# Waiting for one row tile at a time at the turn to the second half of the rows

## The chip, the cores and the metric

The kernel runs on the 8 cores of one Trainium2 chip, in two dies of four. Each core computes 1024 of the 8192 rows; the weights are worked up on every core, and no core waits for another. The metric is device time in microseconds, of the slowest core, from one launch.

## The reference, cut to what matters

```python
def attn(x, w1, w2, b2, sparse_mask):
    a = jnp.einsum('ds,td->st', w1, w2) * sparse_mask          # 4096 x 4096
    return jax.nn.gelu(jnp.einsum('bds,st->bdt', x, a) + b2, approximate=False)

def ffn(x, qweight, scales, scaled_zeros, bias):
    w = (qweight * scales + scaled_zeros).reshape(4096, 4096)   # groups of 128
    return jnp.einsum('bsi,oi->bso', x, w) + bias

x = x + 0.5 * ffn(layernorm(x), ...)
x = x + attn(layernorm(x), ...)
x = x + 0.5 * ffn(layernorm(x), ...)                            # x: 1 x 8192 x 4096, f32
```

## The kernel before

**Two stages.** The first, up to about 1350 us, makes the two weight matrices in bf16 in DRAM: amat, the masked product of w1 and w2, and wdqT, the dequantised and transposed qweight. The second, which the change touches, runs the three layers over the core's rows.

**The second stage.** The loop over u takes 512 rows at a time, as NT = 4 tiles of 128 rows (index j) that lie side by side in x_sb, 4096 f32 columns each. There is one x_sb; both halves use it. Per u three passes p follow one another: p = 0 and p = 2 are the ffn, p = 1 is attn. A pass is a LayerNorm of the four tiles and then matmuls in 8 output blocks (oc) of 512 columns. In the matmuls the four tiles have a PSUM bank each, with 32 products of 128x128 by 128x512 per tile and block for p = 0 and 2; the moving operand mv is double buffered, 4 MB in each half.

**The LayerNorm of one tile.** ScalarE makes the sum of x in p = 0 (L503, a copy with an accumulator) and of its squares (L510), each over 4096 columns, and, after three small instructions of VectorE, the square root (L516). VectorE takes the reciprocal (L618), writes the normalised tile into h_tmp (L623) and then copies 32 transposed blocks from PSUM to hT (L634), while TensorE transposes them (L546), four blocks ahead at most. h_tmp is single, so tile j+1 is normalised when tile j is transposed. ScalarE runs ahead: it works on tile j+1 when its square root of tile j is done. TensorE's first matmul of a pass (L566) waits for all 128 copies, for mv_ld and for the PSUM banks.

**The turn from u = 0 to u = 1.** The last evictions of u = 0 (L648) finish x_sb tile by tile. In SyncE's queue stand four stores of y (L481), each behind the eviction of its tile, each with a semaphore of its own, st_o[j]. Behind them stand the loads of mv for u = 1 (L472); the first two wait for nothing that is not yet done. GpSimd has four loads of the next x tiles into the same places (L428), each behind a wait for its st_o[j]. All four increment one semaphore, x_ld2, by 16 each. ScalarE waits at j = 0 for x_ld2 at 64, and likewise, then without effect, at j = 1 to 3.

Of the kernel before, what the change touches and what calls it, by code (L numbers as in the profile page):

```python
# [24 lines left out]
def A_base(u, p, j):  # L25
    return u * 28 + sum(4 * cA(q) for q in range(p)) + j * cA(p)

def V_base(u, p, j):
    return u * 68 + sum(4 * cV(q) for q in range(p)) + j * cV(p)
# [4 lines left out]
def G_base(u, p):  # L34
    return (u * 3 + p) * 8

def E_base(u, p):
    return (u * 3 + p) * 32
# [79 lines left out]
def build_nc():  # L118
# [21 lines left out]
    def sem1(name):  # L140
        return es.enter_context(nc.semaphore(name))

    def semn(name, n):
        return [es.enter_context(nc.semaphore(f"{name}{i}")) for i in range(n)]
# [23 lines left out]
    mk_ld = semn("mk_ld", 2)  # L168
    p1_st = semn("p1_st", 2)
    x_ld = sem1("x_ld")  # L170
    x_ld2 = sem1("x_ld2")
    st_o = semn("st_o", 4)
    mv_ld = semn("mv_ld", 2)

    with es:
# [7 lines left out]
        with nc.Block() as block:  # L183
            from contextlib import ExitStack as _ES

            with _ES() as es_1:
# [154 lines left out]
                @block.scalar  # L341
                def _(s):
                    acts = []
                    for qq, (sb, tc) in enumerate(P_PAIRS):
                        if TC_FIRST[qq]:
                            acts.append((K_BEFORE[qq], 0, qq))
                    for r in range(32):
                        acts.append((QW_POS[r] + 4, 1, r))
                    for _, kind, idx in sorted(acts):
                        if kind == 0:  # L350
                            qq = idx
                            tc = P_PAIRS[qq][1]
                            sl2 = (qq % 2) * NC * 512
                            s.wait_ge(wt_ld[qq % 2], WT_CNT[qq])
                            s.dma_start(
                                out=w2b.rearrange("(c p) t -> p c t", p=128)
                                    [:, :, tc * 512:(tc + 1) * 512],
                                in_=w2t[:, sl2:sl2 + NC * 512]
                                    .rearrange("p (c t) -> p c t", t=512),
                            ).then_inc(wb_st[tc], 16)  # L360
                        else:
                            r = idx
                            s.wait_ge(wqev, 32 * (r + 1))
                            s.dma_start(out=wdqT.rearrange("(c p) o -> p c o", p=128)
                                        [:, :, r * 128:(r + 1) * 128],
                                        in_=asm2[:, (r % 2) * D:(r % 2) * D + D]
                                        .rearrange("p (c o) -> p c o", o=128)
                                        ).then_inc(q_st[r % 2], 16)
# [43 lines left out]
            with _ES() as es_2:  # L412
# [11 lines left out]
                @block.gpsimd  # L424
                def _(g):
                    for j in range(NT):
                        g.wait_ge(st_o[j], 16)
                        g.dma_start(  # L428
                            out=x_sb[:, j * D:(j + 1) * D],
                            in_=x_in[512 + j * 128:512 + (j + 1) * 128, :],  # L430
                        ).then_inc(x_ld2, 16)

                @block.sync
                def _(sync):
# [54 lines left out]
                @block.scalar  # L489
                def _(s):  # L490
                    for _tc in range(8):
                        s.wait_ge(wb_st[_tc], 16)
                    for u in range(2):
                        for p in range(3):
                            for j in range(NT):
                                a0 = A_base(u, p, j)
                                v0 = V_base(u, p, j)
                                s.wait_ge(ac_ln, a0)
                                if p == 0:
                                    s.wait_ge(x_ld if u == 0 else x_ld2, 64)  # L500
                                    if u == 1:
                                        s.wait_ge(p2_ev, 96)
                                    s.activation(sq_scr[:], x_sb[:, j * D:(j + 1) * D],  # L503
                                                 AF.Copy,
                                                 accum_out=stats[:, j:j + 1]
                                                 ).then_inc(ac_ln, 1)
                                    s.wait_ge(ac_ln, a0 + 1)
                                else:
                                    s.wait_ge(p2_ev, E_base(u, p - 1) + 29 + j)
                                s.activation(sq_scr[:], x_sb[:, j * D:(j + 1) * D],  # L510
                                             AF.Square,
                                             accum_out=stats[:, 4 + j:5 + j]
                                             ).then_inc(ac_ln, 1)
                                tvar_idx = 3 if p == 0 else 4
                                s.wait_ge(ve_ln, v0 + tvar_idx)
                                s.activation(stats[:, 16 + j:17 + j],  # L516
                                             stats[:, 4 + j:5 + j],
                                             AF.Sqrt,
                                             bias=stats[:, 12 + j:13 + j],
                                             scale=1.0 / D).then_inc(ac_ln, 1)  # L520
                            if p == 1:
                                for oc in range(8):
                                    for j in range(NT):
                                        l = oc * 4 + j
                                        s.wait_ge(p2_pe, G_base(u, 1) + oc + 1)
                                        if l >= 2:
                                            s.wait_ge(p2_ev, E_base(u, 1) + l - 1)
                                        s.activation(  # L528
                                            gel[:, (l % 2) * 512:(l % 2) * 512 + 512],
                                            psb[j][:],  # L530
                                            AF.Gelu).then_inc(p2_gl, 1)
# [153 lines left out]
```

## Time and profile before

| | us |
|---|---|
| median of 2 runs | 3017.17 (3008.67 and 3025.67) |
| the profiled execution | 3009.43 |
| its span on the slowest core, core 6 | 3007.9 |
| TensorE busy, matmuls | 1872.3 |
| VectorE busy | 755.8 |
| ScalarE busy | 168.3 |
| first instruction of the second stage on ScalarE | 1349 |
| turn to u = 1, last eviction to first matmul | about 2144 to 2245 |

A span runs from the first to the last instruction of a core. Busy times are sums over one engine; a line number names the line of the kernel from which an instruction came. "Idle before, released by" tells what an engine had waited for. "Us to landing" is the time of a DMA from its issue until its last byte has arrived, so that issue plus this time is the moment at which its semaphore is complete.

### The profile page before, as it was taken

What the parts mean: (1) busy time and instruction counts of PE and PEld (TensorE: products, weight loads), DVE (VectorE), ACT (ScalarE), POOL (GpSimd) and SP (SyncE); (2) the same over time, 40 slices, a digit from 0 to 9 for tenths busy, and PEclk for the clock granted to TensorE, in tenths of its full rate; (3) what the DMA queues carried; (4) which work ended last, traced back from release to release, by engine and by line L of the source; (5) the groups of instructions that cost most, each with busy time, mean ns of one, the idle gap of its engine ahead of it and who ended that gap; (6) DMA issues with size and microseconds to landing.
All of it is one profiled execution on the core that took longest, in us unless ns stands there. A gap on an engine that the chain in (4) does not pass through costs nothing.

```text
span 3007.9 us, 25494 instructions; the slowest of 8 cores (2980.3 to 3007.9 us)
## 1 busy us (share of the span) xinstructions
PE 1872.3 (62%) x8280; PEld 844.1 (28%) x8280; DVE 755.8 (25%) x3395; ACT 168.3 (6%) x157; POOL 83.1 (3%) x124
## 2 busy tenths in 40 slices
PE   0554166340755506736899665999449986758996
PEld 0222023120322202313333322333124333223332
DVE  0033144330553413634100425000040004241000
ACT  0000000000000000003000212000040002130000
POOL 1000000000000000000000000000000000000000
PEclk9977577665776757766889676999759996768898
DMA  9998989999799898962342023333553330241442
GB/s 157 188 173 192 175 116 163 143 216 157 110 161 182 200 170 129 187 194 89 126 144 77 16 71 112 112 112 112 176 160 112 112 113 22 65 121 62 144 130 112
DMA packets 402702, 399.49 MB, mean 133 GB/s; under 512 B 135696, under 2 KB 370992, under 8 KB 396432
## 3 DMA queue, kind: packets, MB, share of 16 engines
q0 software_dynamic: 57856, 117.37, 25.5%
q1 hardware_dynamic: 180240, 213.39, 23.8%
q10 hardware_dynamic: 164480, 67.11, 10.6%
q8 instruction: 72, 1.18, 0.2%
q14 instruction: 54, 0.44, 0.1%
HBM read 407.47 MB, written 91.10 MB: 166 GB/s over the span
## 4 chain that ended last, share of the span: by engine, by line
PE 50%; DMA 15%; another core or an unknown queue 15%; DVE 13%; issue 5%; ACT 2%; DVEq 1%; SPq 0%; ACTq 0%; POOLq 0%
PE ps L566 37%; DMA amat<-aev 8%; PE pa L400 8%; DMA mkt<-mask 4%; DVE x_sb L648 3%; DVE wout L309 3%; DVE asm L333 2%; DVE hT L634 2%; PE tr L546 2%; DVE h_tmp L623 2%; PE ptr L379 2%; PE ps L576 2%; DMA x_sb<-x_in 1%; DMA y_out<-x_sb 1%
## 5 line engine op out<-in xcount | busy, mean ns | idle before, releaser
L566 PE MATMUL ps<-mv,hT 128*128 128x512 bf16 x4536 | 1098.8, 409 | 142.0 <-DVE x_sb L648 137.4
L566 PEld LDWEIGHTS ps<-mv,hT 128*128 128x128 bf16 x4536 | 467.0, 104 | 772.0 <-issue 312.9
L400 PE MATMUL pa<-w2t,w1blk 128*128 128x512 bf16 x1760 | 441.1, 416 | 351.7 <-DMA w1blk<-w 240.6
L379 PE MATMUL ptr<-ident_bf,wout 128*128 128x128 bf16 x1024 | 163.1, 241 | 363.5 <-DVE asm L333 352.1
L400 PEld LDWEIGHTS pa<-w2t,w1blk 128*128 128x128 bf16 x1760 | 182.5, 105 | 596.8 <-issue 429.3
L648 DVE SCALAR_TENSOR_TENSOR x_sb<-ps,x_sb 128x512 f32<-128x512 f32 x128 | 80.8, 687 | 1007.5 <-PE ps L576 1007.5
L546 PE MATMUL tr<-ident_bf,h_tmp 128*128 128x128 bf16 x768 | 131.6, 264 | 255.3 <-DVE h_tmp L623 242.4
L309 DVE TENSOR_SCALAR wout<-qt,scl_sb,zro_sb 128x128 bf16<-128x128 bf16 x1024 | 234.0, 318 | 26.0 <-DMA qt<-qw 26.0
L321 DVE TENSOR_TENSOR aev<-pa,mkt 128x512 bf16<-128x512 f32 x55 | 37.8, 689 | 729.7 <-PE pa L400 435.1
L379 PEld LDWEIGHTS ptr<-ident_bf,wout 128*128 128x128 bf16 x1024 | 100.2, 100 | 431.2 <-issue 395.0
L333 DVE COPY asm<-ptr 128x128 bf16<-128x128 bf16 x1024 | 165.5, 218 | 42.2 <-DMA wdqT<-asm 20.8
L546 PEld LDWEIGHTS tr<-ident_bf,h_tmp 128*128 128x128 bf16 x768 | 80.3, 105 | 308.1 <-issue 288.5
L634 DVE COPY hT<-tr 128x128 bf16<-128x128 bf16 x768 | 124.0, 219 | 35.0 <-PE tr L546 18.4
L510 ACT ACTIVATE sq_scr<-x_sb 128x4096 bf16<-128x4096 f32 x24 | 86.8, 3616 | 563.3 <-DVE x_sb L648 560.5
L648 DVE SCALAR_TENSOR_TENSOR x_sb<-gel,x_sb 128x512 f32<-128x512 f32 x64 | 41.7, 690 | 172.5 <-ACT gel L528 172.5
L503 ACT ACT_TABLE_LOAD x1 | 1.3, 1283 | 1349.2 <-DMA x_sb<-x_in 1349.2
L232 POOL DMA_DIRECT2D amat<-aev x55 | 30.3, 550 | 1156.2 <-DVE aev L321 853.7
L623 DVE TENSOR_SCALAR h_tmp<-x_sb,stats 128x4096 bf16<-128x4096 f32 x24 | 57.9, 2412 | 4.6 <-DVE stats L618 4.6
L503 ACT ACTIVATE sq_scr<-x_sb 128x4096 bf16<-128x4096 f32 x8 | 28.9, 3616 | 332.7 <-DMA x_sb<-x_in 331.6
L528 ACT ACTIVATE gel<-ps 128x512 f32<-128x512 f32 x64 | 36.4, 596 | 156.1 <-PE ps L576 149.0
L576 PE MATMUL ps<-fb_bf,halves_bf 1*128 1x512 bf16 x128 | 33.0, 377 | 0.0
L603 DVE TENSOR_SCALAR stats<-stats 128x1 f32<-128x1 f32 x24 | 3.6, 151 | 116.4 <-ACT sq_scr L510 115.1
(32 smaller groups left out, 134.9 us busy)
## 6 DMA issues: line engine op xcount, KB each, us to landing
mv<-wdqT SPq DMA_DIRECT2D x32, 4096.0 KB, 14.0
w1blk<-w POOLq DMA_DIRECT2D x16, 2048.0 KB, 55.1
w2t<-w2T POOLq DMA_DIRECT2D x8, 4096.0 KB, 59.4
w2b<-w2t ACTq DMA_DIRECT2D x8, 4096.0 KB, 44.1
qt<-qw POOLq DMA_DIRECT2D x32, 1024.0 KB, 16.0
wdqT<-asm ACTq DMA_DIRECT2D x32, 1024.0 KB, 13.5
w2t<-w2b SPq DMA_DIRECT2D x6, 4096.0 KB, 49.5
y_out<-x_sb SPq DMA_DIRECT2D x8, 2048.0 KB, 16.1
```

The lines of the kernel that those rows point to most:

```text
L309: v.tensor_scalar(wout[:, sl * D + gg * 128: sl * D + gg * 128 + 128], qt[:, sl * D + gg * 128: sl * D + gg * 128 + 128], scl_sb[:, r * 32 ...
L321: v.tensor_tensor(aev[:, (k % 2) * 512:(k % 2) * 512 + 512], pa[k % 2][:], mkt[:, (k % 2) * 512:(k % 2) * 512 + 512], op=ALU.mult,).then_i ...
L333: v.tensor_copy(asm2[:, (r % 2) * D + blk * 128: (r % 2) * D + blk * 128 + 128], ptr[b % 4][:],).then_inc(wqev, 1)
L379: t.transpose(ptr[b % 4][:], wout[:, (r % 2) * D + blk * 128: (r % 2) * D + blk * 128 + 128], ident_bf[:]).then_inc(wqtr, 1)
L400: ins = t.matmul(pa[k % 2][:], w1blk[:, dc * 1024 + st * 128: dc * 1024 + st * 128 + 128], w2t[:, (qq % 2) * NC * 512 + dc * 512: (qq % 2) ...
L510: s.activation(sq_scr[:], x_sb[:, j * D:(j + 1) * D], AF.Square, accum_out=stats[:, 4 + j:5 + j]).then_inc(ac_ln, 1)
L546: t.transpose(trp[tg % 4][:], h_tmp[:, ic * 128:(ic + 1) * 128], ident_bf[:]).then_inc(p2_tr, 1)
L566: t.matmul(psb[j][:], hT[:, ic * 512 + j * 128: ic * 512 + j * 128 + 128], mv[:, sl + ii * 512:sl + ii * 512 + 512], start=(ii == 0), stop ...
L576: ins = t.matmul(psb[j][:], lrow[0:1, :], brow[0:1, oc * 512:(oc + 1) * 512], start=False, stop=True,)
L623: v.tensor_scalar(h_tmp[:], x_sb[:, j * D:(j + 1) * D], stats[:, 8 + j:9 + j], stats[:, 20 + j:21 + j], op0=ALU.subtract, op1=ALU.mult).th ...
L634: v.tensor_copy(hT[:, ic * 512 + j * 128: ic * 512 + j * 128 + 128], trp[tg % 4][:],).then_inc(p2_trv, 1)
L648: v.scalar_tensor_tensor(x_sb[:, j * D + oc * 512: j * D + oc * 512 + 512], src, 1.0, x_sb[:, j * D + oc * 512: j * D + oc * 512 + 512], o ...
```

## The change

The one semaphore of the four loads becomes four, and ScalarE waits at tile j for the load of tile j alone. The first half of the rows keeps its single wait for all four tiles. Nothing else differs; loads, stores and their order are as before.

```diff
-    x_ld2 = sem1("x_ld2")
+    x_l2 = semn("x_l2", 4)
...
                             in_=x_in[512 + j * 128:512 + (j + 1) * 128, :],
-                        ).then_inc(x_ld2, 16)
+                        ).then_inc(x_l2[j], 16)
...
                                 if p == 0:
-                                    s.wait_ge(x_ld if u == 0 else x_ld2, 64)
+                                    if u == 0:
+                                        s.wait_ge(x_ld, 64)
+                                    else:
+                                        s.wait_ge(x_l2[j], 16)
                                     if u == 1:
                                         s.wait_ge(p2_ev, 96)
```

## Rows read from the trace of the kernel before

**Rows 1.** Spans and granted TensorE clock of the cores, slowest and fastest

```profile
core 5: 2980.3 us, clock 0.768
core 6: 3007.9 us, clock 0.764
```

**Rows 2.** Chain that ended last, core 6: start us, us, what

```profile
2180.68 13.94 DMA x_sb<-x_in
2194.76 3.72 ACT sq_scr L503 x2
...
2245.13 29.53 PE ps L566 x128
```

**Rows 3.** Timeline, core 6, GpSimd: start us, us, instruction [idle before]

```profile
2151.61 0.54 POOL L428 DMA_DIRECT2D x_sb<-x_in  x1 [844.86 <-DMA y_out<-x_sb]
2160.23 0.54 POOL L428 DMA_DIRECT2D x_sb<-x_in  x1 [8.09 <-DMA y_out<-x_sb]
2170.74 0.53 POOL L428 DMA_DIRECT2D x_sb<-x_in  x1 [9.96 <-DMA y_out<-x_sb]
2180.68 0.53 POOL L428 DMA_DIRECT2D x_sb<-x_in  x1 [9.41 <-DMA y_out<-x_sb]
```

**Rows 4.** Timeline, core 6, SyncE's queue: the first two mv loads, same columns

```profile
2146.20 55.64 SPq L472 DMA_DIRECT2D mv<-wdqT  x2
```

**Rows 5.** DMA issues, core 6 (x tiles, then mv): us to landing last

```profile
x_sb<-x_in POOLq DMA_DIRECT2D x1, 2048.0 KB, 18.5
...
x_sb<-x_in POOLq DMA_DIRECT2D x1, 2048.0 KB, 19.7
...
x_sb<-x_in POOLq DMA_DIRECT2D x1, 2048.0 KB, 16.2
...
x_sb<-x_in POOLq DMA_DIRECT2D x1, 2048.0 KB, 13.9
...
mv<-wdqT SPq DMA_DIRECT2D x1, 4096.0 KB, 64.9
```

**Rows 6.** Timeline, core 6, ScalarE: the starts of tiles 1 and 3

```profile
2203.64 3.62 ACT L503 ACTIVATE sq_scr<-x_sb 128x4096 bf16<-128x4096 f32 x1 [0.20 <-ACT stats L516]
...
2224.82 3.62 ACT L503 ACTIVATE sq_scr<-x_sb 128x4096 bf16<-128x4096 f32 x1 [0.20 <-ACT stats L516]
```

**Rows 7.** Timeline, core 6, VectorE: tile 0, then tile 1

```profile
2202.37 0.15 DVE L603 TENSOR_SCALAR stats<-stats 128x1 f32<-128x1 f32 x1 [57.99 <-ACT sq_scr L510]
...
2203.88 2.41 DVE L623 TENSOR_SCALAR h_tmp<-x_sb,stats 128x4096 bf16<-128x4096 f32 x1 [0.18 <-DVE stats L618]
...
2212.99 0.14 DVE L603 TENSOR_SCALAR stats<-stats 128x1 f32<-128x1 f32 x1
```

**Rows 8.** Stretches, core 6, first LayerNorm: busy us, PEclk, DMA share, GB/s

```profile
1362.00:1373.00 11.00, 5.85 (x36) 3.69 (x36) 8.23 (x40) 8.54 (x6) 0.00 (x0) 0.50 1.07 343
1373.00:1384.00 11.00, 5.84 (x34) 3.40 (x33) 8.46 (x40) 7.91 (x7) 0.00 (x0) 0.50 0.07 23
```

**Rows 9.** Core 1: loads of tiles 0, 1, us to landing, ScalarE's start

```profile
2129.43 0.54 POOL L428 DMA_DIRECT2D x_sb<-x_in  x1 [832.61 <-DMA y_out<-x_sb]
2134.58 0.54 POOL L428 DMA_DIRECT2D x_sb<-x_in  x1 [4.61 <-DMA y_out<-x_sb]
...
x_sb<-x_in POOLq DMA_DIRECT2D x1, 2048.0 KB, 18.7
...
x_sb<-x_in POOLq DMA_DIRECT2D x1, 2048.0 KB, 25.9
...
2178.41 3.62 ACT L503 ACTIVATE sq_scr<-x_sb 128x4096 bf16<-128x4096 f32 x1 [331.68 <-DMA x_sb<-x_in]
```

**Rows 10.** Stretches, core 6, first matmuls behind the LayerNorm (L566)

```profile
2245.00:2246.00 1.00, 0.87 (x3) 0.35 (x4) 0.50 0.00 0
2250.00:2254.00 4.00, 4.00 (x21) 1.77 (x19) 1.00 0.00 0
```

**Rows 11.** Waits, core 6, 2245 to 3008 us, the longest: total, times, longest

```profile
DVE x_sb L648 <- PE ps L576: 503.2, 16, 31.7
```

## The prediction

> **What bounds the kernel now.** I read the spans of all cores first, then the page's part with slices of the span, then the chain of work that ended last around the turn from the first 512 rows to the second, and then the timelines of the queues in that stretch. The cores differ by under 1% in span, at one clock [rows 1], so the time is that of core 6 and every core can be argued alike. Behind 1350 us TensorE is what the kernel is made of, except at one place: the turn. There the chain leaves TensorE, goes through a store of y, then through the last load of x, then to ScalarE, and returns to the matmuls at 2245.1 us [rows 2]. The edit touches what ScalarE waits for in exactly this chain.
>
> The turn on core 6 runs so. GpSimd issues the four x loads one by one, each as the store of the same tile has landed: at 2151.6, 2160.2, 2170.7 and 2180.7 us [rows 3]. Two mv loads of 4 MB stand in SyncE's queue from 2146.2 us on, and share the DMA engines with them [rows 4]. The x loads take 18.5, 19.7, 16.2 and 13.9 us [rows 5], and so land at 2151.6+18.5 = 2170.1, 2160.2+19.7 = 2179.9, 2170.7+16.2 = 2186.9 and 2180.7+13.9 = 2194.6 us. ScalarE starts on tile 0 at 2194.8 [rows 2], 0.2 us behind the fourth landing: the wait for 64 is what held it, although its own tile had been there for 24.5 us.
>
> **What the change removes.** Tile 0 no longer waits for tiles 1 to 3. It can start at 2170.1+0.2 = 2170.3 us: 2194.8-2170.3 = **24.5 us** earlier. The rest of the LayerNorm follows tile 0 in a fixed order, one tile behind the other, and the question is whether the later tiles are there in time.
>
> ScalarE's first pass over tile 1 started at 2203.6 and over tile 3 at 2224.8 us [rows 6]; 24.5 us earlier these are 2179.1 and 2200.3. Tile 1 lands at 2179.9, so it is 0.8 us late. Tile 1 has room for that: ScalarE needs 2202.4-2194.8 = 7.6 us for its two passes over a tile [rows 2, 7], so it was through with tile 1 at 2203.6+7.6 = 2211.2, while VectorE, busy with tile 0, took it up at 2213.0 [rows 7]: 1.8 us of slack, more than 0.8. Tile 2, between them, was started half the way from tile 1 to tile 3, at about 2214.2; 24.5 us earlier that is 2189.7, and it lands at 2186.9, 2.8 us early. Tile 3 lands at 2194.6, 5.7 us early. So what sets the pace is VectorE, with one tile in about 10.6 us (2213.0-2202.4), and the whole row of work shifts by the full 24.5 us.
>
> **Does it keep its pace?** It now runs while x and mv are still landing, where before its second half had the DMA engines idle. The first LayerNorm of the kernel shows both: in the stretch with a DMA share of 1.07 VectorE was busy 8.23 us of 11.0, in the next, at a share of 0.07, 8.46 us of 11.0, with 40 instructions in each [rows 8]. DMA traffic doesn't stretch these instructions; I take zero. The bound above: 0.2 us in 11, or 1 us over the 50.4 us from 2194.8 to 2245.1.
>
> **What is late next.** At 2245.13-24.5 = 2220.6 us TensorE wants the first mv tile. It was issued at 2146.2 [rows 4] and landed 64.9 us later [rows 5], at 2211.1: 9.5 us to spare. The change issues no DMA and moves none, so this landing stays.
>
> **What it adds.** Three more waits on ScalarE, one for each of tiles 1 to 3. Behind each of them, in ScalarE's order, stand the two passes of the same tile and its square root, and behind those VectorE's normalisation, the transposes and so the matmuls. All of them need that tile anyway. The cost of a wait that is already met: nothing to a tenth of a microsecond (tile 1 started 0.2 us behind the square root in rows 6), covered by the slack above. Four semaphores in place of one: nothing that the trace would show. The wait on p2_ev for 96 is met at the end of the evictions, before the first load is issued.
>
> **The other cores.** Core 1 issued its first two x loads at 2129.4 and 2134.6; they took 18.7 and 25.9 us, and ScalarE started at 2178.4 [rows 9]. Tile 0 had landed at 2148.1, so it may gain 30.1 us with the same 0.2 us of wake-up. Tile 1, though, lands at 2160.5, and is wanted 8.9 us behind tile 0's start (2203.6-2194.8 on core 6), at 2157.2: 3.3 us late, 1.8 us of it covered, 1.5 lost. Core 1 gains 28.6. Core 6 was the last to reach the turn and its loads had the least company; it has the smallest gain and stays the last.
>
> **The sum.** 24.5 us off the span of core 6: 3007.9-24.5 = 2983.4. The profiled execution took 3009.43 us, 1.5 more than its span: 2984.9 us. One of the two runs shown is at 3008.67, like it, the other at 3025.67, and their median is 3017.17. I take the middle between the profiled execution and the median, 3013.3, as the base, and so 3013.3-24.5 = **2989 us**, 0.9% below the median. About 2%, some 60 us, is what a measurement of this kernel can tell from no change; by that measure this is no change.
>
> **Rivals.**
> *The fourth load is held up by VectorE.* New is that VectorE works on tile 0 while GpSimd still has a load to issue. VectorE's normalisation of tile 0, 2.41 us long from 2203.9 [rows 7], moves to 2179.4 to 2181.8, and the issue at 2180.7 falls into it. If the load had to wait for its end, it would come 1.1 us later, of the 5.7+1.8 = 7.5 us to spare: no loss. If it waited until VectorE is through with tile 0, at 2213.0-24.5 = 2188.5, it would land at 2202.4, 2.1 us late, 0.3 of it uncovered. If through tile 1 also (10.6 more), 10.9 us are lost: 3000 us. Against it: in the trace of before nothing of the sort is seen, as VectorE idled then. The Trainium skill, page "SBUF — State Buffer", section "Who interferes with whom", has a rule for it: a VectorE instruction in a two-port mode keeps GpSimd from a port that both use, for its whole length, and a DMA issued from GpSimd then waits for its descriptors. No row here shows it; by that rule the sum would be the first or the second of these cases, 2989 us either way. Chance of a loss of over 5 us: 5%.
>
> *mv gates the matmuls.* It would have to land 9.5 us later than it did. Each microsecond beyond costs one; at 10 beyond the time is 2999 us. For it speaks only that its landing is far longer than an undisturbed one, against it that all that it shares the engines with is issued at the same times as before. 3%.
>
> *TensorE's clock (the one that ends on the other side).* Its idle time at the turn shrinks. VectorE had idled 58.0 us ahead of tile 0 [rows 7], which becomes 33.5, and TensorE somewhat longer in both cases; its work ahead of the matmuls is the same. The first matmuls behind the LayerNorm ran at 0.50, the 1.2 GHz level, and within 5 us at 1.00, the 2.4 GHz level [rows 10]; so the first group of 128 took 29.5 us [rows 2], of which some 25 at the full clock. A group that stayed at the lower level would take 25 us more. One such group eats the gain (3013.3-24.5+25 = 3014 us), and from the fourth on (+100-24.5, 3089) the kernel is slower by over 2%. Nothing speaks for it: TensorE idles in both versions and starts its transposes at the lower level in this trace, and goes through the same 128 transposes. 2%.
>
> *The gain is lost later.* A later wait for a DMA would absorb it. The waits after 2245 us name none; the longest is VectorE's for the matmuls, 503.2 us [rows 11]. The stores at the end follow the last evictions. That the change does nothing at all (tile 0 in truth landing with tile 3) is against the landings of rows 5. Together 3%: about 3013 us.
>
> **Chances and range.** Forecast 87%, the four rivals 5, 3, 2 and 3%. Low end: the lowest run, 3008.67, less core 1's 30.1 and 3 us of spread: 2975. High end: the highest run less the gain is 3001, the first two rivals give 3000; with 5 us of spread, 3006. The cases beyond hold 5%, run-to-run spread perhaps 10 more. Faster by over 2% would need 36 us more than the turn holds here: 2%. Slower by over 2%: 2%. Within: 96%.
>
> **What would show it.** In the profile after, ScalarE's first L503 of the second half starts 0.2 us behind the landing of tile 0, some 24 us before the fourth lands; L503 waits for a DMA at tile 1, for about 1 us or a few on cores like core 1, and hardly at tiles 2 and 3; the four tiles keep 10.6 us each; TensorE's idle stretch ahead of the transposes shrinks by the same 24 us; the first matmul of the second half still waits for VectorE's hT and not for mv; the fourth load is issued and lands as before. The prediction would be wrong if the chain at that matmul named mv, if the fourth load took clearly over 14 to 19 us, or if the first matmul group took over 31 us.

## The result, and the profile after

The changed kernel took 2983.9 us, the median of 15 runs, against 3009.85 us for the kernel before in 14 runs of the same comparison: a ratio of 0.9909, with a 95% interval of 0.9876 to 0.9942. That is 26 us between the medians and 27 us by the ratio (17 to 37). A second comparison on another occasion, the run `again` below, gave 0.993 (0.9888 to 0.9971), some 21 us (9 to 34). The gain is clear of zero in both and short of 2%. All ratios leave out the runs in which the cores of a die ran at a lower TensorE clock (2 of the 15 here, one of the two of `sp_loads`, four of the seven of `cols_tail`), and since the profiles of `cols` and `cols_tail` below are of such runs, only the turn and the end, which come out alike on both dies, are read from them.

The profiled execution took 2978.37 us. Its spans, as in [rows 1]:

```profile
core 0: 2976.6 us, clock 0.767
...
core 6: 2964.1 us, clock 0.769
```

Core 0 ended last, not core 6. The chain of core 0 at the turn, start us, us, what, answering to [rows 2]:

```profile
2134.19 8.54 DMA y_out<-x_sb
2143.30 18.89 DMA x_sb<-x_in
2162.32 3.72 ACT sq_scr L506 x2
...
2212.69 29.58 PE ps L569 x128
```

The chain now runs over the store and the load of tile 0, where it ran over the last load. From the first load's issue it is 2143.3+18.9 = 2162.2 us, and ScalarE starts 0.1 us later. ScalarE's four first passes, as in [rows 6]:

```profile
2162.32 3.62 ACT L506 ACTIVATE sq_scr<-x_sb 128x4096 bf16<-128x4096 f32 x1 [307.58 <-DMA x_sb<-x_in]
...
2172.42 3.62 ACT L506 ACTIVATE sq_scr<-x_sb 128x4096 bf16<-128x4096 f32 x1 [1.41 <-DMA x_sb<-x_in]
...
2181.81 3.62 ACT L506 ACTIVATE sq_scr<-x_sb 128x4096 bf16<-128x4096 f32 x1 [0.20 <-ACT stats L519]
...
2192.39 3.62 ACT L506 ACTIVATE sq_scr<-x_sb 128x4096 bf16<-128x4096 f32 x1 [0.20 <-ACT stats L519]
```

The brackets tell what ended each wait: the DMA for tile 0, the DMA for tile 1 (1.41 us, where the start could have come 1.2 us sooner), and for tiles 2 and 3 only the square root ahead of them. VectorE, as in [rows 7]:

```profile
2169.94 0.15 DVE L606 TENSOR_SCALAR stats<-stats 128x1 f32<-128x1 f32 x1 [33.99 <-ACT sq_scr L513]
...
2180.55 0.14 DVE L606 TENSOR_SCALAR stats<-stats 128x1 f32<-128x1 f32 x1
...
2191.13 0.14 DVE L606 TENSOR_SCALAR stats<-stats 128x1 f32<-128x1 f32 x1
```

It idled 34.0 us ahead of tile 0 instead of 58.0, and takes up a tile every 10.6 us as before. No bracket stands at tiles 1 and 2: ScalarE's lateness with tile 1 did not reach it. So it is on cores 0, 2, 4 and 6, where VectorE's steps stay within 0.2 us of 10.6. On cores 1, 3, 5 and 7 tile 1 came later, and on 1, 3 and 7 tile 2 too: VectorE's steps there were 11.5 to 12.0 us and then 10.7 to 11.5, and the way from ScalarE's start to the first matmul took 51.5 to 52.7 us instead of 50.4 to 51.0.

For comparing runs I use the **turn**: from the issue of the first y store of the turn (L481) to the first matmul of the second half (L566, in the changed kernel L569), worked out for each core from the timelines. On core 0 after it is 2212.69-2134.19 = 78.5 us; on core 6 before 2245.1-2142.6 = 102.5.

| kernel | turn: shortest, median, longest core |
|---|---|
| before | 102.5, 106.4, 106.9 |
| changed | 76.9, 78.5, 80.6 |

Core by core the turn is shorter by 25.4 us (core 0), 27.8 (core 1), 24.6 (core 6) and 29.6 (core 7); the others lie between 26 and 29.

### The profile page after: what moved, and what is told of

Its sections match the earlier page's. It is cut to its first block, busy times and chain, and to the rows that moved or that the text cites. A ratio compares the mean times of both kernels' runs of the same rounds, so it can differ in the third digit from the quotient of the medians.

```text
span 2976.6 us, 25494 instructions; the slowest of 8 cores (2937.6 to 2976.6 us)
## 1 busy us (share of the span) xinstructions
PE 1873.3 (63%) x8280; PEld 844.5 (28%) x8280; DVE 753.8 (25%) x3395; ACT 168.3 (6%) x157; POOL 83.9 (3%) x124
## 3 DMA queue, kind: packets, MB, share of 16 engines
q10 hardware_dynamic: 164480, 67.11, 10.7%
## 4 chain that ended last, share of the span: by engine, by line
PE 50%; another core or an unknown queue 15%; DMA 14%; DVE 13%; issue 5%; ACT 2%; DVEq 1%; SPq 0%; ACTq 0%; POOLq 0%
PE ps L569 37%; PE pa L400 8%; DMA amat<-aev 7%; DMA mkt<-mask 5%; DVE x_sb L651 3%; DVE wout L309 3%; DVE asm L333 2%; DVE hT L637 2%; PE tr L549 2%; DVE h_tmp L626 2%; PE ptr L379 2%; PE ps L579 2%; DMA x_sb<-x_in 2%; ACT sq_scr L513 1%
## 5 line engine op out<-in xcount | busy, mean ns | idle before, releaser
L569 PE MATMUL ps<-mv,hT 128*128 128x512 bf16 x4536 | 1099.9, 409 | 141.9 <-DVE x_sb L651 137.3
L569 PEld LDWEIGHTS ps<-mv,hT 128*128 128x128 bf16 x4536 | 467.2, 104 | 772.7 <-issue 314.1
L637 DVE COPY hT<-tr 128x128 bf16<-128x128 bf16 x768 | 121.5, 219 | 36.7 <-PE tr L549 18.3
```

Source lines behind the costliest of these rows:

```text
L569: t.matmul(psb[j][:], hT[:, ic * 512 + j * 128: ic * 512 + j * 128 + 128], mv[:, sl + ii * 512:sl + ii * 512 + 512], start=(ii == 0), stop ...
L637: v.tensor_copy(hT[:, ic * 512 + j * 128: ic * 512 + j * 128 + 128], trp[tg % 4][:],).then_inc(p2_trv, 1)
```

## The experiments

Eight kernels ran. Times scatter by more than the differences looked for, since the cores come out of the first stage at times that differ from run to run (in `again` their first y stores were issued between 2050.8 and 2148.5 us, in the kernel before between 2117 and 2143), and the time is that of the last core. So the turn, which is read on eight cores in each profile, decides, and the ratio only confirms.

**The changed kernel again**, as a yardstick. No edit.

> The changed kernel once more, as the yardstick of this group. Turn means here: from the issue of the first y store of the first half to the first matmul (L569) of the second half. Theory (the turn is tile 0's landing plus a LayerNorm that VectorE paces at 10.6 us a tile): turn 77 to 81 us on every core, against 102 to 107 in the kernel before; time 24 to 29 us under the kernel before. Rival (part of the gain was luck of the cores' start times): turn shortened, but a time within 10 us of the kernel before.

Measured: turn 73.4, 76.2 and 77.2 us (shortest, median, longest), ratio 0.993 (0.9888 to 0.9971). The gain is there again, at some 21 us a little under the 24 to 29 expected. What I had not expected is how short the turn was on most cores, 73.4 us on core 7 and 73.8 on core 0: below my 77 to 81. The four x loads of core 7 took 15.9, 19.9, 15.2 and 11.5 us, where those of core 0 in the first profile took 18.9, 20.7, 17.1 and 15.1.

Core 7 came to its turn 24 us ahead of any other core, but that is not the reason. Core 3 had three others within 25 us of it, and its loads took the same 15.9, 19.9, 15.2 and 11.6 us. What both have is a distant neighbour in the pairs 0/1, 2/3, 4/5 and 6/7 (47 and 44 us later). Over the 48 cores of the six profiles in which GpSimd issues whole tiles, the four times add up to 78.9 to 89.6 us on all 17 cores whose neighbour began its turn between 3 us before and 21 us after them, and to 62.4 to 74.7 us on all 31 others. Six other ways to pair the cores (0/2, 0/4, 0/7 and so on) do not part them so.

**Tile 0 waits for tile 1 as well.**

```diff
                                         s.wait_ge(x_l2[j], 16)
+                                        if j == 0:
+                                            s.wait_ge(x_l2[1], 16)
```

> Tile 0 waits for its own load and for that of tile 1; tiles 2 and 3 as in the changed kernel. Theory: ScalarE starts at tile 1's landing, 10 to 12 us behind that of tile 0, all behind it shifts by as much: turn 88 to 91 us, time about 10 us over the changed kernel, some 15 under the kernel before. Rival (mv or the DMA traffic sets the turn, and tile 0's start only fills slack): turn under 84 us, time within 5 us of the changed kernel.

Measured: turn 82.3, 88.5 and 89.5 us, ratio 0.9955 (0.9912 to 0.9999), which by itself does not stand apart from that of `again`. The median turn is 12.3 us longer than that of `again`, which ran on the same chip, and ScalarE started 32 to 39 us behind the first store, where it started after 23 to 27. On core 4, the last of this run:

```profile
2182.73 3.62 ACT L508 ACTIVATE sq_scr<-x_sb 128x4096 bf16<-128x4096 f32 x1 [318.62 <-DMA x_sb<-x_in]
...
2191.61 3.62 ACT L508 ACTIVATE sq_scr<-x_sb 128x4096 bf16<-128x4096 f32 x1 [0.20 <-ACT stats L521]
...
2202.22 3.62 ACT L508 ACTIVATE sq_scr<-x_sb 128x4096 bf16<-128x4096 f32 x1 [0.20 <-ACT stats L521]
```

Only the first start waits for a DMA. What tile 0 waits is paid nearly in full at the first matmul: in the mean of the eight cores ScalarE starts 12.7 us later than in `again` and the turn is 12.1 us longer, since some cores of `again` had lost a little at tile 1. The rival (under 84 us) holds on no core but core 2, whose neighbour was 38 us behind it; against core 7 of `again` (73.4 us), whose neighbour was far off too, it lost 8.9 us, where ScalarE's start lost 9.2 (32.2 instead of 23.0).

**The first mv load ahead of the stores.** The load leaves its place in the loop behind the stores.

```diff
+                                if g == 24:
+                                    continue
...
+                        if u == 0:
+                            sync.wait_ge(p2_pe, 23)
+                            sync.dma_start(out=mv[...], in_=wdqT[...]).then_inc(mv_ld[0], 16)
                         for j in range(NT):
                             sync.wait_ge(p2_ev, E_base(u, 2) + 29 + j)
```

> The first mv load of the second half is issued ahead of the four y stores, when its buffer comes free at the end of matmul group 23, so that 4 MB less are moved in the turn. Theory: in SyncE's ring mv stood behind the stores and took nothing from tile 0's load; tile 0 lands 28 us behind the first store as before (within 1 us), turn 77 to 81 us, time as the changed kernel. Rival (mv shares the DMA engines with tile 0's load and holds it up): tile 0 lands 2 to 5 us sooner, turn and time shorter by as much.

Measured: turn 73.4, 75.7 and 78.3 us, ratio 0.9949 (0.9909 to 0.999). ScalarE started 23.0 to 27.8 us behind the first store, in `again` 23.0 to 26.5. On core 1 here and core 7 of `again` the loads took 15.9, 19.9, 15.1 and 11.5 against 15.9, 19.9, 15.2 and 11.5 us: the same without 4 MB of mv. mv takes nothing from tile 0. The trace before says why. On core 6 SyncE's queue moved this from 2142.6 us, the first store's issue, to 2180.6, where the fourth store had landed (packets, MB, share of the 16 engines):

```profile
q1 hardware_dynamic: 605, 8.42, 65.6%
```

8.42 MB are the four stores of 2.1 MB, all but 0.03, so mv, issued at 2146.2, had hardly begun. The prediction had it share the DMA engines with all four x loads.

**mv held until tile 3 has landed.**

```diff
+                                if g == 24:
+                                    sync.wait_ge(x_l2[3], 16)
                                 if g >= 2:
                                     sync.wait_ge(p2_pe, g - 1)
```

> The changed kernel, with SyncE's first mv load of the second half held until tile 3 of x has landed. Theory (mv has some 9.5 us of slack in the changed kernel, and stood behind the stores): tile 0's landing stays within 1 us, 23 to 28 us behind the first store; mv is issued 52 to 55 us behind the first store and needs 14 to 24 us, so it lands at 67 to 78, and the turn stays at 74 to 80 us. Rival (mv is the gate and slows x): x lands 3 us sooner or more, or the first matmul waits for mv and the turn moves with mv's landing.

Measured: turn 74.1, 76.5 and 78.5 us; one run, 2996.2 us. On core 7, which ended last, SyncE's queue behind the stores:

```profile
2204.14 10.93 SPq L474 DMA_DIRECT2D mv<-wdqT  x2
```

and TensorE's first matmuls of the second half:

```profile
2232.49 29.58 PE L571 MATMUL ps<-mv,hT 128*128 128x512 bf16 x128 [0.69 <-DVE hT L639]
```

The first mv load landed 20.2 us after its issue, at 2224.3, still 8 us ahead of the matmul, which waited for hT alone. x landed no sooner (ScalarE's start after 23.6 to 27.9 us). So mv is not the gate even when it is issued 50 us behind the first store, and its long landing in [rows 5] was a place in a queue behind the stores, and then a small part beside the last x load (0.68 MB from 2180.6 to 2194.6 us), not a slow transfer.

**The x loads in SyncE's queue, between the stores.** The four loads leave GpSimd.

```diff
+                            if u == 0 and j >= 1:
+                                x_load(j - 1)      # waits for st_o[j - 1], then loads the tile
+                        if u == 0:
+                            x_load(3)
```

> As the kernel with the early mv load, and the four x loads are issued from SyncE's queue in between the stores: store 0, store 1, load 0, store 2, load 1, store 3, load 2, load 3, each load behind its own store's landing. 2 MB take about 6.2 us at the 340 GB/s of the turn. Theory (tile 0's load was slow since it shared the DMA engines with stores 1 to 3): tile 0 lands after three transfers, some 20 us behind the first store instead of 28, tile 3 after eight, at about 52, just in time for its turn on ScalarE; turn 70 to 74 us, time 5 to 8 us under the changed kernel. Rival (a store's landing costs more than its transfer, so the ring runs empty between them): turn 78 us or more, no gain.

Measured: turn 69.8, 74.6 and 78.2 us, ratio 0.9889 (0.9825 to 0.9954), which does not stand apart from that of `again`. The first half of the expectation held on the five cores that did best: ScalarE started after 18.2 to 20.1 us; on the other three after 22.5 to 23.7. The second half did not: ScalarE's starts on tiles 1 and 2 came 9.8 to 14.7 us behind the tile ahead, where VectorE takes one in 10.6, so part of what tile 0 gained was lost at tiles 1 and 2. The median turn is 1 to 2 us shorter than in `again`, `mv_early` and `mv_late`, not 5 to 8. The rival, a queue that runs empty between stores and loads, is not what the trace of core 0 shows: the DMA engines moved 364 to 427 GB/s in each stretch up to 2130 us. The slip was in the expectation. Tile 1 lands after five transfers and tile 2 after seven, by its own 6.2 us each at 31 and 43 us, where ScalarE, started at 19, would take them up at 28 and 38. It had counted only tiles 0 and 3.

**The x loads in SyncE's queue, behind all stores.**

```diff
+                        if u == 0:
+                            for j in range(4):
+                                x_load(j)
```

> As the kernel with the early mv load, and the four x loads are issued by SyncE behind all four stores, not by GpSimd. Theory: in one ring the loads stand behind the stores, tile 0 lands after five transfers of 6.2 us, some 33 us behind the first store instead of 23 to 28, the later tiles 6 us apart, so none is late; turn 82 to 86 us. The fourth load's issue, which took up to 2.6 us on GpSimd against 0.5 us for the others, shows no such growth beside VectorE. Rival (GpSimd's way of issuing costs more than the sharing of the engines): tile 0 lands sooner than with GpSimd, turn under 76 us.

Measured: turn 78.8, 81.7 and 85.7 us; time 3025.4 us, from one run. Tile 0's start moved to 28 to 35 us behind the first store, and the tiles behind it were in time on every core (8.9, then 10.6 us apart). The median is 6 us worse than with the early mv load alone. Loads from GpSimd's queue, beside the stores, land tile 0 sooner than loads that stand in line behind them (23 to 28 us against 28 to 35). SyncE's load issues took 0.33 to 0.34 us each, but none of them met the normalisation of tile 0, so the expectation's last point was not put to the test here. In `inter1`, on core 7, SyncE issued an mv load 0.2 us into a normalisation (h_tmp from 2133.52 us, the issue at 2133.73), and it took 0.39 us, as on the other cores.

**Stores and loads by blocks of columns.** In the last pass of the first half each block of 512 columns of y is stored when its matmul block has been evicted, and x of the second half is loaded into its place; for the turn only the eighth block of each tile is left. ScalarE waits at every tile for all seven block loads (x_c at 112) besides its x_l2[j].

```diff
+                                if (u, p) == (0, 2) and oc >= 1:
+                                    cb = oc - 1
+                                    sync.wait_ge(p2_ev, E_base(u, 2) + 4 * oc)
+                                    sync.dma_start(out=y_out[..., cb], in_=x_sb[..., cb]).then_inc(st_c[cb], 16)
...
+                    for oc in range(7):
+                        g.wait_ge(st_c[oc], 16)
+                        g.dma_start(out=x_sb[..., oc], in_=x_in[512:1024, oc]).then_inc(x_c, 16)
```

> The changed kernel, with y of the first half stored and x of the second half loaded in blocks of 512 columns, each when its matmul block has been evicted; only the eighth block is left for the turn, tile by tile. Theory (tile 0's landing plus a LayerNorm of 50.4 us): the last block of a tile is 256 KB, stored and loaded in 3 to 4 us each, ScalarE starts 6 to 10 us behind the first store of the turn, tiles 1 to 3 are never late, turn 57 to 61 us, 17 to 20 us under the changed kernel, time 42 to 46 us under the kernel before. Rival (next gate is mv, whose load now lands alone but is issued behind the stores, or the blocks of 2 KB rows disturb the mv loads of the last pass): turn over 65 us or matmul groups apart by more than 34.2 us.

Measured: turn 59.8, 60.2 and 64.2 us, ratio 0.9843 (0.978 to 0.9906), a gain of 47 us (28 to 66) on the kernel before, whose median on that occasion was 3020.7. The interval of the ratio overlaps that of the changed kernel; the turn is what sets the two apart. The median turn is 16 us shorter than in `again`. ScalarE starts 9.6 to 13.6 us behind the first store, later than the 6 to 10 expected. From there it is 50.1 to 50.8 us on every core: the theory's floor, a LayerNorm of 50.4 us behind the landing of tile 0, with nothing else in it. The rivals did not occur: no turn was over 65 us, and on core 5 the last pass's matmul groups were 34.1 us apart, under 34.2.

**The same, and the second half's y by columns too.** The last four stores of the second half shrink to the eighth block as well.

```diff
-                                if (u, p) == (0, 2) and oc >= 1:
+                                if p == 2 and oc >= 1:
```

> As the kernel with the stores and loads by column block, and the second half's y is stored by column block too, so that 1 MB in place of 8 MB is left to store behind the last eviction. Theory: the turn as there, 57 to 61 us; from the last eviction's end to the end of the span 3 to 6 us instead of some 18 to 20; time 55 to 62 us under the kernel before. Rival (small row pieces of 2 KB slow the stores, and the end is set by a fixed time of a store and its receipt): tail over 10 us.

Measured: turn 59.7, 60.4 and 62.7 us; ratio **0.9744** (0.9681 to 0.9807), a gain of 77 us (58 to 96) on the kernel before, from three runs. It is the fastest of all and beats the changed kernel; its interval overlaps that of `cols`. The 77 us are more than the 55 to 62 expected and than turn and end show (46 and 18 to 20), but the interval holds both. From the end of the last weight matmul (L566 in the kernel before) to the end of the span it is 6.2 to 6.3 us on every core, against 23 to 27 in all kernels without this edit. The chain at the turn on its slowest core, core 0:

```profile
2178.63 2.46 DMA y_out<-x_sb
2181.66 6.62 DMA x_sb<-x_in
2188.41 3.72 ACT sq_scr L531 x2
```

The store of tile 0's last block takes 2.5 us and its load 6.6, where those of the whole tile took 8.5 and 18.9 in the changed kernel.

## Why the prediction was right

**What the wait held back.** The step "tile 0 can start when it has landed" held to a tenth: 24.5 us were forecast for core 6, and its turn is 24.6 us shorter; core 1 was given 28.6 and shows 27.8. The kernel `two` gives the same step its slope: tile 0's start put off by 9.2 us, on cores with no neighbour near, cost 8.9.

**Slack of the later tiles.** Forecast for core 6 was that tile 1 is 0.8 us late and hidden. On core 0 it was 1.2 us late, and VectorE took tiles 1 and 2 up 10.6 us apart without a wait. "What sets the pace is VectorE" does not hold on every core, though. On core 1 ScalarE started 30.1 us earlier, as forecast, but 2.3 us were lost behind it and not 1.5, because tile 2 was late too (ScalarE waited 2.8 us for it), which the prediction did not work out. On core 3 the chain at the turn runs over the store and the load of tile 2, not of tile 0. The four cores that lose so are those whose pair neighbour follows 8 to 16 us behind. The prediction's reason for core 6's quick loads, "the least company", was near: it is one core that counts, its neighbour, which was 15 us ahead.

**VectorE's pace beside DMA traffic.** Forecast to stay, with 1 us as the bound. It stayed where the tiles were there in time: h_tmp 2.41 us, 10.6 us a tile.

**mv's slack.** 9.5 us were forecast for core 6. On core 0 the load, issued at 2137.8, took 65.4 us, landed at 2203.2 and was wanted at 2212.7: 9.5. On the other cores it was 7.6 to 10.6 us, and in `again` 5.0 to 18.9. That the landing "stays" was right, though not its picture of mv sharing the engines from its issue on. The row, as in [rows 5]:

```profile
mv<-wdqT SPq DMA_DIRECT2D x1, 4096.0 KB, 65.4
```

`mv_late` showed that mv is in time even when its load waits for all of x.

**The clock.** The first matmul group took 29.6 us on core 0 and 29.3 to 30.4 on the others, against 29.5 in [rows 2]; the third rival did not occur.

**The fourth load beside VectorE.** Here the rival's mechanism is real and its price is nil, as the first of its cases had it. GpSimd's queue on core 0, answering to [rows 3]:

```profile
2143.30 0.54 POOL L428 DMA_DIRECT2D x_sb<-x_in  x1 [844.99 <-DMA y_out<-x_sb]
2151.54 0.54 POOL L428 DMA_DIRECT2D x_sb<-x_in  x1 [7.70 <-DMA y_out<-x_sb]
2162.56 0.53 POOL L428 DMA_DIRECT2D x_sb<-x_in  x1 [10.47 <-DMA y_out<-x_sb]
2172.65 1.33 POOL L428 DMA_DIRECT2D x_sb<-x_in  x1 [9.56 <-DMA y_out<-x_sb]
```

and VectorE's normalisation of tile 0 in the same timeline:

```profile
2171.45 2.41 DVE L626 TENSOR_SCALAR h_tmp<-x_sb,stats 128x4096 bf16<-128x4096 f32 x1 [0.18 <-DVE stats L621]
```

The fourth issue takes 1.33 us in place of 0.53 and ends at 2173.98, 0.12 us behind the end of h_tmp at 2173.86. In `again`, core 0, they began within 0.1 us of each other; GpSimd's queue:

```profile
2124.38 2.63 POOL L428 DMA_DIRECT2D x_sb<-x_in  x1 [9.32 <-DMA y_out<-x_sb]
```

and VectorE:

```profile
2124.48 2.41 DVE L626 TENSOR_SCALAR h_tmp<-x_sb,stats 128x4096 bf16<-128x4096 f32 x1 [0.18 <-DVE stats L621]
```

2.63 us, to 2127.01; h_tmp ended at 2126.89, again 0.12 earlier. It is so on all 13 cores of the changed kernel, `again`, `mv_early` and `mv_late` whose fourth issue was prolonged (0.59 to 2.63 us): each ends 0.11 to 0.13 us behind h_tmp. Where h_tmp had ended by 0.33 us into the issue, or began 0.19 us or more after it, the issue took 0.53 us, and in `two`, where tile 0 comes too late to meet it, it took 0.53 us on all eight cores. The trace agrees with the rule of the Trainium skill, page "SBUF — State Buffer", section "Who interferes with whom". VectorE's copies from PSUM (L637), which begin 0.6 us behind and keep it busy for 5.9 us, held no issue that met them (on cores 4 and 5 of `again` h_tmp had ended 1.2 and 1.0 us before the issue and the copies were running: 0.53 us), so the second and third cases of that rival fall. The load still landed in time: on core 0 at 2172.65+15.1 = 2187.8 us, wanted at 2192.4. The closest was core 0 of `again`, where it took 19.8 us, with 2.63 for the issue and the neighbour just arrived: landed at 2144.2, wanted at 2145.5.

**The sum.** Forecast were 2989 us from a base of 3013.3; the base by more runs is 3009.85, and the medians differ by 26 us, not 24.5. "Core 6 stays the last" was wrong: core 0 ended last in the profile after, and others in other runs, since the order in which the cores come out of the first stage is not fixed. It costs the sum little, because the turn's gain is 24.6 to 29.6 us on every core. That the forecast came within 5.1 us of the median is in part luck: the base was a middle taken from one profile and the median of two runs, and it was 3.5 us too high where runs of one kernel scatter by 30 and more. The two profiled executions differ by 31.1 us, and not all of it is the change. From core 6 before to core 0 after, the last of each, the turn is 24.0 us shorter (102.5 and 78.5), the first store of the turn came 8.4 us earlier (2142.6 and 2134.2), which the change does not explain, and what follows the turn took 1.1 us longer.

## What to carry to other kernels

Where several loads increment one semaphore and the consumer takes them one by one, look at the landing of the first and of the last: their distance is what a semaphore for each can give, provided that the consumer's pace per piece is slower than the pace of arrival, and that the next input (here mv) has landed by the new time. Ask it of every core: in the changed kernel VectorE waited a microsecond or so for a later piece on just the cores whose pair neighbour was close behind. The deeper cure is not to wait more finely but to leave less to move: the same stores and loads, spread over the matmuls ahead by column blocks, took another 16 us from the turn and 17 from the end.

## What the runs showed of the hardware

A DMA issue on GpSimd that meets VectorE's normalisation of a 128x4096 f32 tile to bf16 is held until that instruction is over (up to 2.63 us in place of 0.53, ended 0.12 us behind it), while VectorE's own instruction stays at 2.41 us. And the cores slow one another's loads in the pairs 0/1, 2/3, 4/5 and 6/7, not as a crowd. The four 2 MB loads of x took 15.9, 19.9, 15.2 and 11.6 us on core 3 of `again`, with three other cores within 25 us but its neighbour 44 us away, and 18.7, 25.6, 25.0 and 19.2 us on core 1 of the changed kernel, whose neighbour began 11 us behind it. Of the 48 cores of six profiles none is out of line. Which resource the two share was not tested.
